# Freeing gathered rows one by one instead of sixteen at a time in a product-key attention stage

## What is computed

```python
kv_scores, indices = _pk(x, Wq_pk, pk_keys)      # top 16 of 64*64 key pairs, softmax over the 16
ind = indices + offsets[None, None, :, None]     # a row number in the table, 16 per token and head
k = jnp.einsum('bnhk,bnhkd->bnhd', kv_scores, keys_table[ind])
v = jnp.einsum('bnhk,bnhkd->bnhd', kv_scores, values_table[ind])
sim = jnp.einsum('bihd,bjhd->bhij', q, k)        # 8 heads, causal
attn = jax.nn.softmax(sim, axis=-1)
out = jnp.einsum('bhij,bjhd->bhid', attn, v)
out = out.transpose(0, 2, 1, 3).reshape(b, n, HEADS * DIM)
return x + out @ Wo                              # the tower adds the layer's input
```

## Time and profile before

| what | value |
|---|---|
| median of 3 runs | 16746.29 us (16664.32 to 16760.74) |
| span of the profiled execution | 16598.0 us |
| PE busy in it | 10426.9 us (63%) |
| DVE | 8776.5 us (53%) |
| ACT | 6776.6 us (41%) |
| GpSimd | 6839.7 us (41%) |
| the last stage, first to last gather | 5364.8 to 16326.0 us |

### The profile page before, as it was taken

The page is one execution under the profiler, slowest core; times in us unless marked ns, Lnnn a source line. Parts: engine busy times, 40 slices in busy tenths (PEclk is TensorE's granted clock), DMA queues, the critical chain, the costliest instruction groups (busy, mean ns, idle before and its releaser), DMA issues.

```text
span 16598.0 us, 138013 instructions
## 1 busy us (share of the span) xinstructions
PE 10426.9 (63%) x38094; PEld 5354.4 (32%) x38094; DVE 8776.5 (53%) x22927; ACT 6776.6 (41%) x14111; POOL 6839.7 (41%) x5848
## 2 busy tenths in 40 slices
PE   1656756646663566666666666666666666666667
PEld 1322222223131233333333333343333333333334
DVE  3538979974856444444444444444444444444441
ACT  0225434421021444544444444444444444444443
POOL 3007757750000544444444444444444444444441
PEclk9757878876775677887777777787777777778776
DMA  0003323320000111111111111111111111111110
GB/s 21 12 3 120 123 90 123 122 77 14 10 7 18 39 39 37 40 38 36 39 39 37 35 40 36 40 37 40 38 35 40 36 41 34 40 37 39 38 36 18
DMA packets 538604, 723.53 MB, mean 44 GB/s; under 512 B 412866, under 2 KB 420593, under 8 KB 503386
## 3 DMA queue, kind: packets, MB, share of 16 engines
q0 software_dynamic: 168448, 338.54, 7.8%
q1 hardware_dynamic: 369418, 376.55, 7.3%
HBM read 697.87 MB, written 8.42 MB: 43 GB/s over the span
## 4 chain that ended last, share of the span: by engine, by line
PE 26%; another core or an unknown queue 19%; ACT 11%; issue 7%; DVE 3%; DVEq 1%; ACTq 0%
PE l3m_acc L2569 6%; PE l3m_O L2540 5%; ACT l3m_spread L2665 4%; PE l3m_S L2523 3%; PE l3m_DX L2559 3%; PE l3m_T L2530 3%; ACT l3m_prob L2694 2%; PE l3m_S L2559 2%; ACT l3m_V L2707 2%; ACT l3m_W L2711 2%; ACT l3m_probT L2703 1%; PE l3m_T L2483 1%; PE l3m_DX L2560 1%; PE l3m_T L2508 1%
## 5 line engine op out<-in xcount | busy, mean ns | idle before, releaser
L2465 POOL DMA_INDIRECT l3m_got<-in_l_table,l3m_row x5120 | 4928.0, 963 | 6110.9 <-ACT l3m_spread L2665 3560.0
L2569 PE MATMUL l3m_acc<-l3m_W,l3m_values 128*128 128x512 f32 x3072 | 2038.9, 751 | 1302.8 <-issue 656.5
L2947 DVE SCALAR_TENSOR_TENSOR tower_h<-l3m_O,l3m_pinv,tower_h 128x64 f32<-128x64 f32 x512 | 145.3, 284 | 3392.4 <-PE l3m_O L2540 2470.2
L2665 ACT ACTIVATE l3m_spread<-l3m_got,l3m_weight 128x128 f32<-128x128 f32 x5120 | 1926.8, 495 | 24.2 <-DVE l3m_kv L2927 12.7
L2703 ACT ACTIVATE l3m_probT<-l3m_T 128x512 f32<-128x512 f32 (+3 forms) x1280 | 684.9, 535 | 2173.6 <-remote 1446.2
L2540 PE MATMUL l3m_O<-l3m_vo_g,l3m_probT 128*128 128x64 f32 x5440 | 864.9, 306 | 901.8 <-ACT l3m_probT L2703 668.2
L1325 POOL TENSOR_TENSOR m_mul<-m_st,m_wide_c 128x2048 f32<-128x2048 f32 x256 | 1158.4, 4525 | 432.3 <-DVE m_st L1598 426.6
L2540 PEld LDWEIGHTS l3m_O<-l3m_vo_g,l3m_probT 128*128 128x128 f32 x5440 | 822.1, 221 | 1161.7 <-ACT l3m_probT L2703 811.1
L2569 PEld LDWEIGHTS l3m_acc<-l3m_W,l3m_values 128*128 128x128 f32 x3072 | 599.5, 225 | 1662.4 <-issue 837.6
L2530 PE MATMUL l3m_T<-tower_ident,l3m_prob 128*128 128x128 f32 x4352 | 846.5, 318 | 400.0 <-issue 242.7
L2711 ACT ACTIVATE l3m_W<-l3m_DX 128x512 f32<-128x512 f32 x971 | 578.0, 595 | 1125.8 <-remote 681.1
(11 more groups left out here) (694 smaller groups left out, 20714.0 us busy)
## 6 DMA issues: line engine op xcount, KB each, us to landing
m_wide_c<-l1a_c SPq DMA_DIRECT2D x256, 1024.0 KB, 4.6
l3m_got<-in_l_table,l3m_row POOLq DMA_INDIRECT x5120
l3m_values<-in_l_table SPq DMA_DIRECT2D x288, 256.0 KB
l0i_img<-in_l_x SPq DMA_DIRECT2D x4, 1024.0 KB, 8.1
l2r_x<-l2a_hT SPq DMA_DIRECT2D x8, 512.0 KB, 5.4
qp_inw<-in_q_inw SPq DMA_DIRECT2D x1, 2336.0 KB, 7.8
l_kept<-l0t_xt,l0t_row POOLq DMA_INDIRECT x128
l1a_c<-m_listf SPq DMA_DIRECT2D x16, 128.0 KB, 4.9
```

The costliest lines, as they stand in the source:

```text
L2465: pool.indirect_dma_start(got[:, unit % GOT, j, :], None, table, bass.IndirectOffsetOnAxis(ap=row[:, unit // QUAD % RING, unit % QUAD, j:j ...
L2569: pe.matmul(acc[:], values[:, tile, :], W[:], start=(tile == 0), stop=(tile == TILES - 1)).then_inc(blended, 1)
L2665: copy = act.activation(spread[:, unit % 2, :, j], got[:, unit % GOT, j, :], ACT.Copy, scale=weight[:, g % RING, t, j:j + 1])
```

## The change

A row's buffer is freed by its own copy. With FREED = 1, every one of ACT's copies increments `parted` (before, each sixteenth one), and GpSimd waits in front of every gather for the copy of the same row four units earlier (before, once in front of a unit for the whole unit). DVE's wait in front of its sum asks for the same copy as before, counted in rows.

```diff
-GOT, RING = 4, 5
+GOT, RING, FREED = 4, 5, 1
...
+        def copies_done(unit, rows):
+
+            return (unit * TOPK + rows) // FREED
...
-                if unit >= GOT:
-                    pool.wait_ge(parted, unit - GOT + 1)
                 for j in range(TOPK):
+                    if unit >= GOT and j % FREED == 0:
+                        pool.wait_ge(parted, copies_done(unit - GOT, j + FREED))
                     pool.indirect_dma_start(got[:, unit % GOT, j, :], None, table,
...
-                    if j == TOPK - 1:
+                    if j % FREED == FREED - 1:
                         copy.then_inc(parted, 1)
...
-                dve.wait_ge(parted, unit + 1)
+                dve.wait_ge(parted, copies_done(unit, TOPK))
```

## The result

The changed kernel takes 15,479.2 us (median of 4 runs, 15,439.6 to 15,505.0), the kernel before on the same chip 16,753.5 us (4 runs): ratio 0.9236, 95% interval 0.9203 to 0.9269, so 1,274 us less. The profiled execution has a span of 15,503.3 us, 1,095 less than the 16,598.0 of the one before.

A forecast was written before the change was run, and what follows sets the result against it. The prediction took PE, paced by semaphore updates held late by long gather trains, as the bound. 1,130 less 90 gives 1,040 us off the 16,598.0 span, about 15,560; with 148 for the median, 15,700 us, range 14,900 to 16,300, chance 0.62.

The forecast's parts named there:

- The bound: PE is the path; its semaphore updates come late from about 8 us into a gather train until 3 us after it.
- The form of the loss, 0.62 x (1.25 k - 5): PE's loss in us for k gathers back to back: 9.3 at k = 16, nothing at k = 4 or less.
- The one share of 35% for every length: PE's busy share from 8 us into a gather train until 3 us after, against 92% from there to the next.
- Trains of 7 rows: GpSimd's back-to-back gathers after the change: 5 to 10 rows, 7 as the middle, saving 4.0 us a unit.
- The 33 trains of some 30 rows behind `found`: Gathers after GpSimd's 33 waits for `found` go out some 30 together, not sixteen: 90 us more lost.
- The increments and waits at nothing: 4800 more ACT increments and 4740 more GpSimd waits were taken to cost 0; upper bound for the increments 600 us.
- Trains of 30 being common: Sign of being wrong: if GpSimd often sends some 30 gathers back to back, the forecast fails.
- The sum: (316 - 33) units x 4.0 us = 1,130, less 90 for the long trains, is 1,040 us gained.
- The ceiling: Ceiling of any gain from PE's held stretches: 9.2 us for each of 316 units, some 2,900 us.
- The rule that I weighed against it: Trainium skill: engine and DMA ports are disjoint, so a DMA slows no compute; by it the change gives 16,746 us.
- The chain's unexplained share: Share of "another core or an unknown queue" in the chain should fall from 19% to about 14%.
- The "remote" waits of L2707: "Remote" waits of ACT's copy of the transposed probabilities (L2703 in the prediction) should fall from 1446 us to some 900.

The follow-up runs named there:

- groups of eight: Changed kernel with FREED = 8, so GpSimd waits and ACT increments at every eighth row: 15,930.7 us, ratio 0.9640 to the kernel before.
- groups of four: Changed kernel with FREED = 4, so GpSimd waits and ACT increments at every fourth row: 15,291.8 us, ratio 0.9237 to the kernel before.
- paced kernel before: Kernel before plus a 128x256 f32 clear by GpSimd, and a wait for it, after each gather: 13,876.5 us, ratio 0.8391.
- four pauses: Kernel before with pauses of 256, 16, none and 128 elements, one for each batch's 80 units: 16,119.5 us, ratio 0.9580.
- four kinds: Kernel before with GpSimd doing row gathers, nothing, half-row gathers or clears, one for each batch's 80 units: 12,552.4 us, ratio 0.9988.

## Why the prediction was right, step by step

**The bound.** Right. PE's late updates were the path where the prediction was made, and the runs with a pause show that the gathers' rate makes them late: same rows, same copies, later gathers, and a sixth of the time gone. Only the name was too narrow, since DVE's drains are late in the same trains. The view that found it was the chain's 19% of "another core" on a program with one core, and after it windows cut along the trains.

**The form of the loss, 0.62 x (1.25 k - 5).** Its direction was right: 91% busy in trains of 3 or 4 rows, 47% and 27% in the held part of the middle and the long ones, groups of eight half as good as singles. The one share of 35% for every length was too simple. And its form in time (a hold begins 8 us into a train) was only a stand-in for a rate: at a pitch of 1.44 us trains of any length pass with PE 80% busy. That was not in the prediction, which thought of looser trains only as "might even gain".

**Trains of 7 rows.** Measured 7.3 on the mean, 5.4 without the long ones. **The 33 trains of some 30 rows behind `found`:** 53, of 29.4 rows, so more than I counted, since a GpSimd that keeps up with ACT arrives at `found` sooner and waits there 62 times in place of 33. In all it waits longer there, as foretold (1603.3 us against 1074.6), but a single wait is shorter, 25.9 us against 32.6. And not all of these trains are new: 21 of 32 rows were there before, which the prediction took for sixteens. Trains above 16 hold 672 rows before and 1,560 after, a third of all, and the formula puts half of the loss that is left on them (1,045 of 2,090 us). Trains of 30 being common was one of the prediction's own signs of being wrong, and they are one train in twelve.

**The increments and waits at nothing.** Right, where it can be seen alone: 0.9999 on a chip without holds. ACT's copies also follow one another as before, three in 1.08 us. The warning of the Trainium skill, "VectorE: DVE Perf Modes", section "The TRN2 errata", on dense increments from several engines, has no counterpart in these runs: 5120 in place of 320 changed nothing there, and groups of four and of one have the same ratio on the others.

**The sum.** 1,040 us foretold, 1,274 measured between the medians, but 1,095 between the two profiled executions (16,598.0 and 15,503.3 us), and what is read from their traces has to be held against that. The prediction's own formula, put to the trains as they came, gives less than it had: 2,930 us lost before and 2,090 after (376 trains of up to 4 rows lose nothing, the 53 long ones most), so 840 us. The sum had no term for the clock, and that is the term that was missing. Windows of the middle of the stage, of the kernel before:

```profile
6000.00:16000.00 10000.00, 6602.74 (x26883) 3556.82 (x26880) 4634.06 (x17393) 4765.73 (x11239) 4453.74 (x4624) 0.79 0.15 38
```

of the changed kernel:

```profile
6000.00:15000.00 9000.00, 6318.22 (x26624) 3435.80 (x27115) 4650.61 (x17458) 4782.40 (x11316) 4510.79 (x4639) 0.83 0.16 42
```

of the paced kernel before:

```profile
6000.00:13500.00 7500.00, 6127.82 (x26759) 3321.91 (x26758) 4630.29 (x17322) 4753.64 (x11212) 5999.07 (x9227) 0.90 0.20 50
```

and of the changed kernel on a chip without holds:

```profile
6000.00:12200.00 6200.00, 5511.55 (x26357) 3079.35 (x26355) 4532.81 (x17047) 4630.49 (x11035) 4465.25 (x4533) 0.96 0.23 60
```

The same work but for 2% of the records in each, and PE's granted clock, a mix of 2.4 GHz (1.00) and 1.2, is 0.79, 0.83, 0.90 and 0.96, while PE is busy 6602.74, 6318.22, 6127.82 and 5511.55 us. The less PE is stopped, the faster its clock in these four, and the shorter its own work. The group of the products, L2573 in the three later ones (719, 686 and 630 ns), stands on the page before as

```profile
L2569 PE MATMUL l3m_acc<-l3m_W,l3m_values 128*128 128x512 f32 x3072 | 2038.9, 751 | 1302.8 <-issue 656.5
```

so 751 to 719 ns is 4%; on the 66% of the stage's 10,950 us that PE is busy, it is some 290 us. That and 840 make 1,130, beside 1,095. The pages split the 1,095 nearly so: PE's idle time falls from 6,171 to 5,411 us, by 760, and its busy time from 10,426.9 to 10,092.7, by 334, part of which is records missing from the second page (37,498 products in place of 38,094). No run isolates the clock. So that 1,040 came within 55 us of the profiled difference is partly luck: the trains were put 200 us too high, and a clock term of some 290 was left out. The other 179 us up to 1,274 are not the change's: the profiled execution before was that much faster against its median than the one after, for which the forecast had allowed 148.

**The ceiling.** 2,900 us was too low as a statement on holds: the chips without them are 4,000 us below. The term counted waiting only, at the clock of a PE that is stopped and started again: in the windows above PE is idle 3,397 us before and 688 in the changed kernel without holds, 2,709 less over nine tenths of the stage and so close to the ceiling, and busy 1,091 less, which the ceiling left out. The paced kernel's 2,666 us stays under it.

**The rule that I weighed against it.** "SBUF — State Buffer" in the Trainium skill, section "SBUF: two separate sides", would have it that gathers slow no engine. On the chips without holds that is what was measured: 12,549 us with and 12,515 without 5120 gathers. On the chip with holds it is not: 16,542 us, and 13,876 after nothing but a pause.

**The details foretold.** The chain's unexplained share: 14% said, 15% measured. The "remote" waits of L2707: 900 us said, 1131.8 measured, too low by a quarter. Waits for ACT many and short: 846, 2.3 us on the mean, but one of 35.9.

## What to carry to other kernels

Where the chain of a one-core program has a large share of "another core or an unknown queue", cut windows along the bursts of some other engine and compare PE's busy share inside and outside; here it was 35% against 92%. An engine that sits behind its own drain only inside those bursts, as DVE did here, is a second sign. Here bursts of indirect gathers were it, and spacing them by 0.2 us (1.44 us in place of 1.25) was worth 16%, twice what shorter bursts gave, for one small clear after each; but on a chip without holds a pause buys nothing and, once GpSimd becomes the bound, costs (12% at 1.66 us). And a kernel whose time differs by a quarter between chips has to be compared with itself on one chip, and a change of this kind on chips of both sorts before it is called a gain.

## What the runs showed that was not expected

The same kernel takes 16,542 and 16,826 us in two jobs on one chip and 12,549 to 12,565 on three others (medians). Nearly all of the difference lies in the last stage: its first row copy starts at 5,452 us in the kernel before and at 5,399 with four pauses, both with holds, and at 5,388 without (four kinds), while a quarter of it takes 2,813 us with holds and no pause, and 1,737 to 1,751 without holds. Between a pitch of 1.33 and one of 1.44 us a quarter falls from 2,634 to 2,216 us. A slope that steep, for 0.11 us more a row, would fit gathers that come only just faster than something behind them can take; no run shows what that is. And thousands of increments by ACT, and of waits and clears of 16 elements by GpSimd, cost nothing measurable on the chips without holds.
